# Turns between row and column transforms through DRAM, with the transform matrices stationary

## What is computed

```python
def _fgm(x, w1, b1, w2, b2, alpha, beta, boost):
    x1 = conv2d(x, w1, b1)
    x2 = conv2d(x, w2, b2)
    x2_fft = jnp.fft.fft2(x2)
    h, w = (x.shape[-2], x.shape[-1])
    fh = jnp.fft.fftfreq(h)[:, None]
    fw = jnp.fft.fftfreq(w)[None, :]
    mask = (jnp.sqrt(fh ** 2 + fw ** 2) > 0.3).astype(jnp.float32)[None, None]
    enhanced = x2_fft * (1.0 + boost[None] * mask)
    out = jnp.abs(jnp.fft.ifft2(x1 * enhanced))
    return out * alpha[None] + x * beta[None]
```

## Time and profile before

| | us |
|---|---|
| median of three runs | 1809.78 (1808.87 to 1812.44) |
| profiled execution, its own time | 1805.41 |
| its span (first to last instruction) | 1803.6 |
| first output convolution starts (L755) | 208.3 |
| three images in the middle, from output convolution to output convolution (856.84, 966.50, 1073.17, 1181.07) | 109.66, 106.67, 107.90 |
| last output convolution starts | 1796.03 |

### The profile page before, as it was taken

The page is one execution under the profiler, slowest core; times in us unless marked ns, Lnnn a source line. Parts: engine busy times, 40 slices in busy tenths (PEclk is TensorE's granted clock), DMA queues, the critical chain, the costliest instruction groups (busy, mean ns, idle before and its releaser), DMA issues.

```text
span 1803.6 us, 32142 instructions
## 1 busy us (share of the span) xinstructions
PE 1549.4 (86%) x11664; PEld 906.3 (50%) x11664; DVE 1364.0 (76%) x2455; ACT 864.2 (48%) x1380; POOL 684.9 (38%) x603
## 2 busy tenths in 40 slices
PE   5789899888989889888998988889888898988884
PEld 3346455464555546445463554546455464555542
DVE  4558778687777878788687777868788786778866
ACT  2344545455454544545455454544545545454533
POOL 3244251634416244251534416134251623416151
PEclk9899999999999999999999999999999999999997
DMA  4011020111102011020111102011020201102020
GB/s 147 1 26 41 26 52 1 43 33 37 39 23 53 0 37 39 25 51 0 43 33 37 39 23 53 0 37 39 25 51 0 58 18 37 39 12 53 0 54 12
DMA packets 19618, 60.23 MB, mean 33 GB/s; under 512 B 6228, under 2 KB 6228, under 8 KB 19204
## 3 DMA queue, kind: packets, MB, share of 16 engines
q1 hardware_dynamic: 19588, 59.83, 13.7%
HBM read 14.04 MB, written 9.02 MB: 13 GB/s over the span
## 4 chain that ended last, share of the span: by engine, by line
DVE 39%; PE 25%; DVEq 16%; issue 7%; ACT 6%; SPq 4%; DMA 3%; ACTq 1%; POOL 0%; POOLq 0%
DVE hv L1090 16%; DVEq L959 7%; DVE nT L929 5%; PE bank L647 5%; PE bank L674 4%; SPq L428 4%; DVE row_max L960 4%; DVEq L965 3%; PE bank L467 3%; PE bank L518 3%; PE bank L489 2%; DMA k_heads<-kC 2%; PE bank L755 2%; DVE score L957 2%; PE bank L577 1%
## 5 line engine op out<-in xcount | busy, mean ns | idle before, releaser
L674 PE MATMUL bank<-act,mats_sb 128*32 128x512 f32 (+11 forms) x2112 | 267.1, 475 | 1.4 <-DVE xs L1026 1.4
L1666 POOL TENSOR_TENSOR score<-score,row_max 128x512 f32<-128x512 f32 x128 | 133.4, 1042 | 306.7 <-DVE row_max L960 305.1
L1350 ACT ACTIVATE fft<-bank 128x512 f32<-128x512 f32 x224 | 168.9, 807 | 125.7 <-PE bank L467 111.8
L1090 DVE SCALAR_TENSOR_TENSOR hv<-hor,mix,hv 128x1024 f32<-128x1024 f32 x128 | 193.8, 1514 | 10.7
L467 PE MATMUL bank<-cons_sb,fft 128*128 128x128 f32 x1280 | 185.4, 306 | 11.8 <-DVE fft L1117 11.8
L1090 DVE SCALAR_TENSOR_TENSOR hv<-ver,mix,hv 128x1024 f32<-128x1024 f32 x144 | 186.9, 1298 | 11.0
L1382 ACT ACTIVATE score<-score 128x512 f32<-128x512 f32 x128 | 80.8, 631 | 225.8 <-POOL score L1666 225.8
L467 PEld LDWEIGHTS bank<-cons_sb,fft 128*128 128x128 f32 x1280 | 172.7, 217 | 31.4 <-DVE fft L1117 17.0
L1677 POOL COPY inv_wide<-row_inv 128x128 f32<-128x128 f32 x128 | 91.8, 717 | 206.7 <-DVE row_inv L966 206.7
L674 PEld LDWEIGHTS bank<-act,mats_sb 128*32 128x32 f32 x2112 | 117.5, 109 | 99.6 <-issue 81.5
L1696 POOL TENSOR_SCALAR hor<-act,cols_sb 128x1024 f32<-128x1024 f32 x16 | 18.0, 1125 | 391.6 <-ACT act L1407 391.6
(11 more groups left out here) (180 smaller groups left out, 2903.9 us busy)
## 6 DMA issues: line engine op xcount, KB each, us to landing
pyr_stack<-pyr SPq DMA_DIRECT2D x192, 144.2 KB, 3.1
x_in<-x_dram SPq DMA_DIRECT2D x16, 512.0 KB, 3.5
k_heads<-kC SPq DMA_DIRECT2D x128, 64.0 KB, 2.4
out_dram<-y_out SPq DMA_DIRECT2D x16, 512.0 KB, 2.8
k_heads<-rel_dram SPq DMA_DIRECT2D x2, 1024.0 KB, 13.0
mats_sb<-mats_dram SPq DMA_DIRECT2D x1, 1978.5 KB, 7.4
z_dram<-z_sb SPq DMA_DIRECT2D x32, 19.1 KB
z_run<-z_dram SPq DMA_DIRECT2D x16, 38.2 KB
```

Source lines behind the costliest of these rows:

```text
L674: last = pe.matmul(grids[32 * d:32 * d + 32, y0 - 16 * k:y1 - 16 * k, x0:x1], w_pyr[:, d, t], act[:, y0 + dy:y1 + dy, x0 + dx:x1 + dx], st ...
L1090: last = dve.scalar_tensor_tensor(hv[:], src, mix[:, a, k:k + 1], hv[:], ALU.mult, ALU.add)
L1350: return act_.activation(dst, src, ACT.Copy)
L1666: pool.tensor_tensor(score[:, j % 3], score[:, j % 3], row_max[:, j % 3].unsqueeze(2).broadcast_to([P, HEADS, WT]), ALU.subtract)\
```

## The change

The three turns leave PE and ACT. After a transform, ACT copies the result as it stands (no `other_order`), SP writes it to a tensor in DRAM, waits for the write, and reads it back in the turned order, in pieces of 128 channels (512 bytes). For that the data must have its pixels in the partitions, so `dft_rows`, `inverse_even` and `inverse_odd` now have the matrix stationary and stream 512, 384 or 128 columns of data (`columns4`). `last_even` and `last_odd` stay `multiply4`, and wait for the transfers in place of ACT's copies. A side with a 32-partition block of the image needs four transfers, one with all 128 partitions one transfer. The pyramid's last steps and `x2_conv` move from slot 1 to slot 0, and `dft_rows` from slot 2 to slot 1. DVE's order is unchanged.

```diff
+        turn_dram = [nc.dram_tensor(name, (SIDE, SIDE, C), F32, kind="Internal")
+                     for name in ("spectrum_dram", "even_dram", "odd_dram")]
...
+            def by_columns(t, w):
+                return bass.AP(t, w * C, [[SIDE * C, SIDE], [4 * C, CH], [1, C]])
+
+            def by_rows(t):
+                return bass.AP(t, 0, [[C, P], [4 * SIDE * C, CH], [1, C]])
+
+            def turn_spectrum(n):
+                sp.wait_ge(h_sb, 2 * n + 2)
+                for w in range(4):
+                    sp.dma_start(by_columns(turn_dram[0], w), chunks(fb)[32 * w:32 * w + 32]).then_inc(spectrum_out, 16)
+                sp.wait_ge(spectrum_out, 64 * n + 64)
+                sp.dma_start(chunks(fa), by_rows(turn_dram[0])).then_inc(spectrum_in, 16)
+
+            def turn_even(n):
+                sp.wait_ge(ae_sb, 2 * n + 2)
+                sp.dma_start(by_rows(turn_dram[1]), chunks(fa)).then_inc(even_out, 16)
+                sp.wait_ge(even_out, 16 * n + 16)
+                for w in range(4):
+                    sp.dma_start(chunks(fc)[32 * w:32 * w + 32], by_columns(turn_dram[1], w)).then_inc(even_in, 16)
...
                 load(n + 2)
                 spread_edge(n)
                 spread_keys(n + 1)
+                turn_spectrum(n)
                 stack_pyramid(n)
+                turn_even(n)
+                turn_odd(n)
                 store(n)
...
-                    multiply4(bank[4 + k], fa, k, con("dft_h")).then_inc(h_ps, 1)
-
-            def turn_spectrum(n):
-                for k in range(2):
-                    pe.wait_ge(h_sb, 2 * n + 2)
-                    turn4(bank[6 + k], fb, k).then_inc(t_ps, 1)
+                    pe.matmul(bank[4 + k][:], con("dft_h"), fa[:, HALF * k:HALF * k + HALF], start=True, stop=True)\
+                      .then_inc(h_ps, 1)
+
+            def columns4(dst, src, k, weights, first):
+                if k == 0:
+                    pe.matmul(dst[:, 0:P], first, src[:, 0:P], start=True, stop=True)
+                    return pe.matmul(dst[:, P:4 * P], weights, src[:, P:4 * P], start=True, stop=True)
+                return pe.matmul(dst[:], weights, src[:, 4 * P:8 * P], start=True, stop=True)
...
-                    pe.wait_ge(t_sb, 2 * n + k + 1)
...
+                    pe.wait_ge(spectrum_in, 16 * n + 16)
+                    columns4(bank[6 + k], fa, k, con("dft_w"), con("dft_w0")).then_inc(w_ps, 1)
...
-                    multiply4(bank[6 + k], fc, k, con("even"), con("even0")).then_inc(ae_ps, 1)
+                    columns4(bank[6 + k], fc, k, con("even"), con("even0")).then_inc(ae_ps, 1)
...
-                    pe.wait_ge(te_sb, 2 * n + k + 1)
+                    pe.wait_ge(even_in, 64 * n + 64)
                     multiply4(bank[6 + k], fc, k, con("idft_h")).then_inc(be_ps, 1)
...
-                    pe.wait_ge(to_sb, 2 * n + k + 1)
+                    pe.wait_ge(odd_in, 64 * n + 64)
                     multiply4(bank[4 + k], fd, k, con("idft_h")).then_inc(bo_ps, 1)
...
-                if j == 1:
-                    pyramid(n, 1, range(6, 9))
-                elif j == 2:
-                    dft_rows(n)
+                if j == 0:
+                    pyramid(n, 1, range(5, 9))
                 elif j == 3:
                     r_even(n)
...
             def conv_late(n, j):
                 if j == 0:
-                    pyramid(n, 1, range(5, 6))
+                    x2_conv(n)
                 elif j == 1:
-                    x2_conv(n)
-                elif j == 2:
-                    turn_spectrum(n)
+                    dft_rows(n)
...
-                    copy(other_order(fb, k), rows_of(bank[4 + k])).then_inc(h_sb, 1)
+                    copy(half(fb, k), bank[4 + k][:]).then_inc(h_sb, 1)
```

84 lines of the change are left out of this document (28 added, 56 removed).

## The result

| | us | ratio to before, 95% interval |
|---|---|---|
| before, median of four runs | 1811.11 (1808.87 to 1814.13) | |
| after, median of four runs | 1851.36 (1840.00 to 1859.19) | 1.0202 [1.0168, 1.0236] |
| after, profiled execution (span) | 1853.52 (1851.7) | |

The change makes the kernel 2.0% slower. The forecast was 1860, and 1855.4 for the profiled execution.

What follows compares the result with a forecast made beforehand. DVE was taken to set the pace; 0.5 + 1.2 + 1.4 = 3.1 us per image, 15 times, plus 3.5 for the last, gave 1855.4 profiled, 1860 median with 4.4 more. Forecast range 1835 to 1890; 8 in 10, 1815 to 1920.

Steps and rivals of the forecast that it cites:

- Part A: Moved pyramid steps and x2_conv in slot 0 delay the scores of pair 3, and so DVE's chain, by 0.5 us per image.
- third rival: Clock's low stretch ends before inverse_even or doesn't come: 1.7 us gained per image, 1793 us in all; chance 0.08.
- Part B: Spectrum's trip through DRAM: 8.9 us, PE idles 3.2 before the column product, clock falls; +1.2 us per image (0 to 1.4).
- Part C: Inverse turns: even trip hidden; at the odd one PE waits 2.3 us, +0.4, lower clock +1.0; together +1.4 per image.
- Hidden trips: All trips through DRAM return in time and the clock doesn't fall: 1819 us; chance 0.20.
- Dear pieces: Transfers in 512-byte pieces cost more, at 60 ns each 1958 us, at 40 ns about 1880; chance 0.19 (over 1890).
- The fall moves: The third rival: low clock over before inverse_even or absent, 1.7 us gained per image, 1793 us; chance 0.08.
- No difference: The fall's gain in half of the images just pays for Part A: 1806 to 1813 us; chance 0.08.

Runs made afterwards that it cites:

- after_warm: The changed kernel with the spectrum as one write and four reads, filler products before both waits, and extra products that hold PE's clock: 1782.7 us.
- moved_warm: moved_only with the extra products that hold PE's clock: 1779.5 us.
- bc_freed: The changed kernel with PE waiting for neither the spectrum's nor the odd half's transfers, which still run, their turns left out of the computation: 1801.9 us.
- moved_only: The kernel before with only the steps moved up a slot, all three turns still transposes: 1798.2 us.
- fill: The changed kernel with overwritten filler products on PE, three before the spectrum's wait and two before the odd one, trips unchanged: 1830.7 us.
- before_warm: The kernel before with extra PE products where its clock falls, and the edge product over all 128 partitions: 1774.8 us.
- c_freed: The changed kernel with the last odd product not waiting for the odd transfers, which still run, that turn left out of the computation: 1850.4 us.

## Why the prediction was right, and where it was not

**What bounds.** Right. DVE sets the pace, and the two dates named, the scores of pair 6 and the second projection, are the two at which DVE now waits: in all fourteen images of the loop, and in none of before. PE's and ACT's savings bought nothing where the clock is held (after_warm has them all and is not faster than moved_warm, which has none). Without that, bc_freed, with the savings and neither wait, has images 0.73 us shorter than moved_only's, in the pieces in which the clock falls, and no shorter time (1801.9 and 1798.2).

**Part A, +0.5.** The delay is there, s0 to s3 is 0.37 longer. The step that failed is "below zero it can't go". That holds for DVE's free time at 898.79, but not for the image: moved_only is 15.6 us faster than before, since the fall of the clock comes 7 us earlier in many images: the prediction had this as its third rival and put nothing for it into the sum. The term is -1 us per image by the medians, in place of +0.5. It is +0.4 only when the clock is held.

**Part B, +1.2.** The trip was forecast at 8.9 and took 9.4. Its parts were both off: the writes 5.0, measured 4.5; the read 3.5, taken from the load's row, measured 5.0. That load goes row by row, this read in pieces of 512 bytes; whether the pieces or their order make the difference, no run separates. PE's wait was 3.2 by the forecast, and 3.59 in the image shown, 3.8 as the mean over the first fifteen images. The price from s3 to s6 is +2.01 us: the term was too small by 0.8. The longer trip is 0.5 of it; where the other 0.3 lies I have not separated. Most of the term is the clock's: in fill, with the trip as it is and no fall there, s3 to s6 is 15.96, and 1.69 of the 2.01 are gone. The low stretch stands behind this wait in all fourteen images. By the section "HAM oscillation" in the Trainium skill, page "TensorE: Matmul & The Clock Gate", whose own case has waits of some 3 to 5 us, the clock is lowered at such a wait each time. With waits of 3.5 us and more here, the trace agrees.

**Part C, +1.4.** The even half is hidden, as forecast. The odd trip is 8.0 (forecast 8.1) and PE's wait 2.2 to 2.5 (2.3). The price is +0.88: the low stretch that was taken for given, since the wait is longer than the 1.80 us of the earlier trace rows, follows it in five images of fourteen only. The waits in the case of "HAM oscillation" in the Trainium skill are longer than this one, so the five of fourteen neither bear that rule out nor contradict it.

**What wasn't in the sum.** Ev to py is 0.42 shorter in after, the third rival's mechanism again, at full strength (8.75) in images 1, 13 and 14 only. The first image, which I had counted as any other, lost 4.3, and the last 6.0, not 3.5. There nothing of a Swin block lies between, PE waited 8.2 us for the spectrum, and DVE 4.4 for the boosted product and 1.3 more than before for the pyramid's. But the wait alone is not its price: bc_freed's last image, without it, takes 80.0 as well, with the clock low from 34 us on and behind a wait of PE for DVE.

**The sum.** 0.37 + 2.01 + 0.88 - 0.42 and the unchanged rest (-0.11) make 2.73 per image, where the forecast had 3.1; with the first and the last, 48.1 in place of 50. The total is right partly by luck, since errors cancel: measured from moved_only, which has part A, the turns cost 53 us and not 2.6 x 15 + 3.5 = 42.5; and part A gave 15.6 where it should have cost 7.5. The profiled execution was forecast at 1855.4 and took 1853.5. The 4.4 us from it to the median did not come: the median of after is 2.2 below its profiled execution.

**The rivals.** *Hidden trips*: no, PE waits for both. The estimate from the Trainium skill, page "DMA: Bandwidth & Descriptors", section "Anatomy of one DMA", whose fit is to another issuing path, was 7.4 us for the trip; the measured 9.4 is 2 us more, and 1.8 of it is the read (3.2 by that fit, 5.0 measured). *Dear pieces*: no. By the pages of the two profiles, 24.1% of 16 x 1851.7 us less the 3953 us of before is 3187 us. Divided by the 98304 added packets of 512 bytes that is 32 ns each, and their own records in the trace have 30 ns at the mean; the bound by the byte (34) was it, not the one by the packet (202). *The fall moves*: not in this kernel on the whole, but it is real, and moved_only and bc_freed (9.22 from ev to py) are it. *No difference*: no.

## What to carry to other kernels

Before a transfer takes the place of work on an engine that doesn't set the pace, ask what waits at its end: here about 3 us of PE work per image were swapped for 6 us of idle PE, and DVE, which had waited there in no image of the loop, now does in each. Where PE runs with gaps, price the clock as a quantity of the whole loop: freeing one wait gave 0, freeing two gave 49 us, and moving steps that save nothing gave 16. The cheapest test is a few products into a bank that is overwritten anyway; on the kernel before they gave 2.1%, and no form of the change has a lower median than before_warm's 1774.8 us.

## What the runs showed of the hardware

- A DRAM tensor written from 128 partitions and read back in pieces of 512 bytes: 512 KB written by one issue, 3.2 us; read by one issue, 5.0; read by four issues, 1.9 for the issues and 3.0 to 3.1 to land. Four writes of 128 KB take 4.5. So one write and four reads are 1.3 us shorter than four writes and one read of the same data.
- A packet of 512 bytes took 30 ns at the mean on its engine (after, all 98304 of them). The pyramid's transfers, now issued right behind the spectrum's read, landed after 5.3 us at the median in place of 3.1, still hidden.
- Waits of PE of nearly the same length (2.23 and 2.38 us, at the same place) are followed by a fall of the clock in one kernel's image and not in another's. In c_freed the clock is low at 86 to 90 us in twelve of fourteen images with no such wait at all. What decides was not found; that it isn't the wait alone is shown.
- With the clock held where DVE depends on PE, thirteen images of after_warm in a row take 105.76 to 105.99 us; before, they went 109.7, 106.7, 107.8 in turn.
